# One-column operations merged on VectorE, the bias on GpSimd, and another order of the last two feed-forward steps in a state-space mixer with a quantized feed-forward network

## What is computed

```python
x = x + ssm_forward(ctx, layernorm(x))      # selective scan, 512 channels x 16 states, gated by silu(z)

def ffn(x):                                 # x = layernorm(x), 2048 rows of 512
    h = silu(bit_linear(x, w_gate)) * bit_linear(x, w_up)      # 512 -> 2048
    h = ln_weight * (h * rsqrt(mean(h * h) + 1e-6))
    return bit_linear(h, w_down)                               # 2048 -> 512
x = x + ffn(layernorm(x))

def bit_linear(x, w):
    s  = 127 / clip(max(abs(x), row), 1e-5)             # one scale for each row
    qx = clip(round(x * s), -128, 127) / s
    sw = 1 / clip(mean(abs(w)), 1e-5)                   # one scale for the matrix
    qw = clip(round(w * sw), -1, 1) / sw
    return qx @ qw.T
```

## Time and profile before

| | before |
|---|---|
| median of 3 runs | 584.28 us |
| profiled execution | 586.31 us |
| its span | 584.4 us |
| PE busy | 541.3 us (93%) |
| LDWEIGHTS (PEld) busy | 404.7 us (69%) |
| DVE busy | 540.5 us (92%) |
| ACT busy | 512.1 us (88%) |
| POOL busy | 464.5 us (79%) |
| chain that ended last | DVE 28%, PE 26%, ACT 17%, POOL 12%, issue 11%, DMA 5% |

### The profile page before, as it was taken

How to read it: one execution, slowest core, us unless ns; L and a number is a source line. 1 busy time by engine, 2 the same in 40 slices (tenths; PEclk the granted TensorE clock), 3 DMA queues, 4 the chain that set the end, 5 groups by cost and what they waited for, 6 DMA issues and landing times.

```text
span 584.4 us, 10287 instructions
## 1 busy us (share of the span) xinstructions
PE 541.3 (93%) x3667; PEld 404.7 (69%) x3684; DVE 540.5 (92%) x820; ACT 512.1 (88%) x755; POOL 464.5 (79%) x184
## 2 busy tenths in 40 slices
PE   5898987999999999999999888998889999999996
PEld 2335476899998989989999888995334444444442
DVE  3999979999999999999999999997998999999873
ACT  1899999999999999989999799998967868778673
POOL 4888374999999899999999999994564765666662
PEclk9999999999999999999999899899999999999998
DMA  9992690221112741127331194234532533424321
GB/s 285 407 364 73 230 309 11 56 65 64 55 55 91 163 117 65 59 63 202 88 98 55 55 228 168 62 128 106 104 65 63 109 81 78 112 65 97 94 54 55
DMA packets 62194, 68.65 MB, mean 117 GB/s; under 512 B 41136, under 2 KB 41136, under 8 KB 59968
## 3 DMA queue, kind: packets, MB, share of 16 engines
q1 hardware_dynamic: 59776, 63.59, 36.3%
q0 software_dynamic: 2368, 4.40, 4.5%
HBM read 50.02 MB, written 8.52 MB: 100 GB/s over the span
## 4 chain that ended last, share of the span: by engine, by line
DVE 28%; PE 26%; ACT 17%; POOL 12%; issue 11%; DMA 5%; SPq 0%; DVEq 0%; POOLq 0%; ACTq 0%
POOL arena L470 11%; ACT arena L682 8%; PE ps L1221 8%; PE ps L1205 6%; ACT arena L607 5%; DVE arena L808 5%; PE ps L1208 4%; PE ps L1263 4%; PE ps L1256 3%; DVE arena L897 3%; DVE arena L985 3%; DMA arena<-arena 2%; DVE bst_x L840 2%; DVE am L954 1%; DMA arena<-x 1%
## 5 line engine op out<-in xcount | busy, mean ns | idle before, releaser
L470 POOL TENSOR_TENSOR arena<-arena 128x2048 f32<-128x2048 f32 x63 | 286.4, 4592 | 13.2 <-DVE arena L897 11.1
L897 DVE TENSOR_TENSOR_SCAN arena<-arena,ps 128x512 f32<-128x512 f32 x256 | 286.7, 1197 | 2.0 <-ACT arena L682 0.5
L682 ACT ACTIVATE arena<-arena,a_neg 128x512 f32<-128x512 f32 x256 | 165.5, 712 | 9.5 <-DVE arena L897 9.2
L1221 PE MATMUL ps<-ident,arena 128*128 128x128 f32 x1024 | 156.0, 276 | 6.7 <-POOL arena L470 3.4
L1221 PEld LDWEIGHTS ps<-ident,arena 128*128 128x128 f32 x1024 | 121.2, 142 | 10.7 <-POOL arena L470 6.2
L504 POOL TENSOR_TENSOR arena<-arena 128x1024 f32<-128x1024 f32 x30 | 71.1, 2371 | 57.2 <-DVE arena L985 57.2
L1256 PE MATMUL ps<-arena 128*128 128x512 bf16 x504 | 112.9, 379 | 2.1 <-DVE arena L985 1.1
L1205 PE MATMUL ps<-arena 128*128 128x128 f32 x768 | 102.3, 276 | 3.4 <-ACT arena L607 2.1
L1208 PE MATMUL ps<-ident,arena 128*128 128x128 f32 x640 | 97.8, 277 | 5.2 <-DVE arena L897 2.9
L607 ACT ACTIVATE arena<-arena,bT 128x512 f32<-128x512 f32 x160 | 102.0, 711 | 0.0
L1205 PEld LDWEIGHTS ps<-arena 128*128 128x128 f32 x768 | 93.3, 192 | 5.2 <-ACT arena L607 2.3
(11 more groups left out here) (121 smaller groups left out, 578.1 us busy)
## 6 DMA issues: line engine op xcount, KB each, us to landing
arena<-w_all SPq DMA_DIRECT2D x16, 1024.0 KB, 9.2
arena<-c_rows SPq DMA_DIRECT2D x64, 256.0 KB, 3.2
arena<-x SPq DMA_DIRECT2D x4, 1024.0 KB, 15.8
w_ternary<-arena SPq DMA_DIRECT2D x8, 512.0 KB, 4.2
arena<-w_ternary SPq DMA_DIRECT2D x8, 512.0 KB, 5.0
arena<-x POOLq DMA_DIRECT2D x4, 1024.0 KB, 10.0
out<-arena SPq DMA_DIRECT2D x16, 256.0 KB, 2.0
arena<-ctx_t SPq DMA_DIRECT2D x4, 512.0 KB, 13.7
```

Source lines behind the costliest of these rows:

```text
L470: nc.gpsimd.tensor_tensor(hs[:, k % RING, :, :], hs[:, k % RING, :, :], c_bc[:, s:s + 1, :].to_broadcast([P, KE, L]), ALU.mult).then_inc(S ...
L682: nc.scalar.activation(dA[:, s, i, :], delta_u[:, b, 0, i, :], ACT.Exp, scale=a_neg[:, i, n:n + 1]).then_inc(S["dA_ready"], 1)
L897: nc.vector.tensor_tensor_scan(out=hs[:, k % RING, i, :], data0=dA[:, k % 2, i, :], data1=ps[:, 4 + i, :], initial=0.0, op0=ALU.mult, op1= ...
L1221: last = mm(ps[:, c, i * P:(i + 1) * P], hs[:, k % RING, i, c * P:(c + 1) * P], ident[:], start=(n == 0 and i == 0), stop=(n == DS - 1), i ...
```

## The change

- `variance`: the Square on ACT now takes `scales[:, t, 1:2]` as its scale from SBUF (the sum of squares then comes out scaled), and one `tensor_scalar` makes the variance of h where two did. In the end part the same is done for `var_end` and `ssq_end`.
- `scale_row`: three one-column instructions behind the reduction in place of five: clip and division by 127 in one, the two weight scales in one of two columns, and the reciprocal of the result, without the product with 127 behind it. The reciprocal itself raises `s1_ready`.
- `bias` of tiles 3 to 15 moves from DVE to POOL, behind `power` and ahead of `weigh`; it waits for POOL's own `power` and for the norm of the tile before. `bn_aggr` on DVE now waits for the bias of the tile before.
- In the last step PE makes the last quarter of gate and up ahead of down of tile 13. DVE multiplies that quarter ahead of the maximum and of q2 of tile 14, ACT makes its silu ahead of the rounding of p2 of tile 14.
- `scale_rows(13)` on ACT moves from step 15 behind the rounding of p2 of tile 15.
- The last tile's rows get a place of their own, `o_end`, and the wait for an earlier store ahead of L1063 is gone.

```diff
@@ -130,6 +130,7 @@
         sq_out = part(120, 4).bitcast(BF16)
+        o_end = part(124, 2)
@@ -378,7 +379,7 @@
                     sp.wait_ge(S["fin_done"], t + 1)
-                sp.dma_start(out_v[:, t, :], o_s[:, t % 2, :]).then_inc(out_stored[t % 2], 16)
+                sp.dma_start(out_v[:, t, :], o_end if t == END else o_s[:, t % 2, :]).then_inc(out_stored[t % 2], 16)
@@ -482,6 +483,12 @@
+            def bias(t):
+                pool.wait_ge(S["rstd_ready"], t + 1)
+                hold(pool, "xn_ready", t)
+                nc.gpsimd.tensor_scalar(bia[:], mv[:, 0:1], rstd2[:, 0:1], -1.0, ALU.mult,
+                                        ALU.mult).then_inc(S["bias_ready"], 1)
+
@@ -519,6 +526,8 @@
                     power(EARLY + t + 1, 0 if tile(t + 3) else 1, 2 if tile(t - 1) else 1)
+                if tile(t + 3):
+                    bias(t + 3)
@@ -735,7 +744,7 @@
                     hold(act, "h_ready", t * 4, "ssq_ready", t - 1)
-                    nc.scalar.activation(sq_out, h2[:, 1 - s, :], ACT.Square,
+                    nc.scalar.activation(sq_out, h2[:, 1 - s, :], ACT.Square, scale=scales[:, t - 1, 1:2],
@@ -748,21 +757,24 @@
                     nc.scalar.activation(sq_out[:, 0:1024], h2[:, END % 2, 0:1024], ACT.Square,
+                                         scale=scales[:, END, 1:2],
                                          accum_out=ssq[:, END:END + 1]).then_inc(S["ssq_ready"], 1)
+                if t == END:
+                    silu(t, 3)
...
                     round_x(t + 2)
-                if tile(t):
+                if tile(t) and t < END:
...
                     norm(t + 3)
-                if tile(t - 2):
+                if tile(t - 2) and t < END:
...
             hold(act, "h_ready", END * 4 + 4)
-            nc.scalar.activation(sq_out[:, 1024:], h2[:, END % 2, 1024:], ACT.Square,
+            nc.scalar.activation(sq_out[:, 1024:], h2[:, END % 2, 1024:], ACT.Square, scale=scales[:, END, 1:2],
@@ -773,6 +785,7 @@
                                      scale=aq[:, END:END + 1]).then_inc(S["tq_ready"], 1)
+            scale_rows(END - 2)
@@ -911,24 +924,16 @@
                     step(nc.vector.bn_stats(bst[:], x_all[:, n, :]))
+                    hold(dve, "bias_ready", n)
...
                     dve.wait_ge(S["ssq_ready"], chain + 1)
-                    own.done(nc.vector.tensor_scalar(var2[:, 1:2], ssq[:, chain:chain + 1], scales[:, chain, 1:2],
-                                                     1.0 / INNER, ALU.mult, ALU.mult))
+                    own.done(nc.vector.tensor_scalar(var2[:, 1:2], ssq[:, chain:chain + 1], 1.0 / INNER, RMS_EPS,
+                                                     ALU.mult, ALU.add))
...
                 if n is not None:
-                    own.done(nc.vector.tensor_scalar(var2[:, 0:1], mv[:, 1:2], LN_EPS, None, ALU.add))
-                if chain is not None:
-                    own.done(nc.vector.tensor_scalar(var2[:, 1:2], var2[:, 1:2], scales[:, chain, 1:2], RMS_EPS,
-                                                     ALU.mult, ALU.add))
-                own.wait()
+                    step(nc.vector.tensor_scalar(var2[:, 0:1], mv[:, 1:2], LN_EPS, None, ALU.add))
                 dve.sem_inc(S["var_ready"], 1)
-
-            def bias(n):
-                dve.wait_ge(S["rstd_ready"], n)
-                nc.vector.tensor_scalar(bia[:], mv[:, 0:1], rstd2[:, 0:1], -1.0, ALU.mult,
-                                        ALU.mult).then_inc(S["bias_ready"], 1)
@@ -952,14 +957,9 @@
                 step(nc.vector.tensor_reduce(out=am[:], in_=xn(x), axis=AX.X, op=ALU.max, apply_absolute_value=True))
-                step(nc.vector.tensor_scalar(am[:], am[:], Q_EPS, None, ALU.max))
-                own.done(nc.vector.reciprocal(s1[:], am[:]))
-                for w in range(2):
-                    own.done(nc.vector.tensor_scalar(scales[:, x, w:w + 1], wmean[:, w:w + 1], am[:], 1.0 / 127.0,
-                                                     ALU.mult, ALU.mult))
-                own.wait()
-                step(nc.vector.tensor_scalar(s1[:], s1[:], 127.0, None, ALU.mult))
-                dve.sem_inc(S["s1_ready"], 1)
+                step(nc.vector.tensor_scalar(am[:], am[:], Q_EPS, 1.0 / 127.0, ALU.max, ALU.mult))
+                step(nc.vector.tensor_scalar(scales[:, x, :], wmean[:, 0:2], am[:], None, ALU.mult))
+                nc.vector.reciprocal(s1[:], am[:]).then_inc(S["s1_ready"], 1)
@@ -994,7 +994,9 @@
                     if b == NB - 1 and n % 4 == 2 and t < EARLY:
-                        bias(t + 1)
+                        dve.wait_ge(S["rstd_ready"], t + 1)
+                        nc.vector.tensor_scalar(bia[:], mv[:, 0:1], rstd2[:, 0:1], -1.0, ALU.mult,
+                                                ALU.mult).then_inc(S["bias_ready"], 1)
@@ -1021,11 +1023,10 @@
                     scale_row(x_row)
-                if tile(t + 3):
-                    bias(EARLY + t + 1)
...
                 if t == END:
+                    gated_up(t, 3)
@@ -1034,19 +1035,14 @@
                     cut_x(x_row)
-                gated_up(t, 3)
                 if t < END:
+                    gated_up(t, 3)
...
             dve.wait_ge(S["ssq_ready"], END + 1)
-            step(nc.vector.tensor_scalar(var_end[:], ssq[:, END:END + 1], scales[:, END, 1:2], 1.0 / INNER, ALU.mult,
-                                         ALU.mult))
-            own.done(nc.vector.tensor_scalar(var_end[:], var_end[:], scales[:, END, 1:2], RMS_EPS, ALU.mult, ALU.add))
+            step(nc.vector.tensor_scalar(var_end[:], ssq[:, END:END + 1], 1.0 / INNER, RMS_EPS, ALU.mult, ALU.add))
             dve.wait_ge(S["ssq_end_ready"], 1)
-            own.done(nc.vector.tensor_scalar(ssq_end[:], ssq_end[:], scales[:, END, 1:2], 1.0 / INNER, ALU.mult,
-                                             ALU.mult))
-            own.wait()
-            step(nc.vector.tensor_scalar(var2[:, 1:2], ssq_end[:], scales[:, END, 1:2], var_end[:], ALU.mult, ALU.add))
+            step(nc.vector.tensor_scalar(var2[:, 1:2], ssq_end[:], 1.0 / INNER, var_end[:], ALU.mult, ALU.add))
@@ -1059,8 +1055,7 @@
             dve.wait_ge(S["down_psum"], TILES)
-            dve.wait_ge(out_stored[END % 2], END // 2 * 16)
-            nc.vector.scalar_tensor_tensor(out=o_s[:, END % 2, :], in0=ps[:, DOWN_BANK[END % 2], :],
+            nc.vector.scalar_tensor_tensor(out=o_end, in0=ps[:, DOWN_BANK[END % 2], :],
@@ -1257,6 +1252,9 @@
+            def turned_by_dma(t):
+                pe.wait_ge(qT_done[t % 2], (t // 2 + 1) * 16)
+
@@ -1276,8 +1274,8 @@
                         gate_and_up(t, j)
-                    if j == 2 and tile(t - 2):
-                        pe.wait_ge(qT_done[t % 2], ((t - 2) // 2 + 1) * 16)
+                    if j == 2 and tile(t - 2) and t < END:
+                        turned_by_dma(t - 2)
@@ -1288,6 +1286,8 @@
             pe.wait_ge(S["h_ready"], END * 4 + 2)
+            turned_by_dma(END - 2)
+            down(END - 2, 0, KI)
```

## The result

The changed kernel takes **589.73 us** (median of 22 runs, 583.45 to 593.77) beside 585.26 us for the kernel before on the same chip (22 runs, 583.67 to 586.6): ratio 1.0065, 95% interval 1.0043 to 1.0086. So it is slower by about 4 us, where 1.8 us less was forecast. A second set of runs gave the same: 589.92 us (7 runs, 586.77 to 591.75), ratio 1.0067 [1.0043, 1.0091].

What follows compares the result with a forecast made beforehand. The prediction took a loop through DVE and ACT (10.61 us per steady step) as the bound. Its terms 0.3 + 0.6 + 0.2 + 0.7 = 1.8 us off the 584.28 median gave 582.5 us, own range 581.7 to 583.2, with rivals 580.4 to 583.9.

Steps and rivals of the forecast that it cites:

- two waited one-column operations at 0.24: `scale_row` on DVE in a steady step: 0.24 for each operation after the reduction, part of 1.92 replacing 2.37, saving 0.45.
- slower: Outcome of a measurably slower kernel: chance 0.05, the worse half of a rival with a second clock fall (+ 3.2, 585.7 us).
- Scan stage, - 0.3: First `scale_row` call, DVE scanning without a gap: 0.30 saved reaches POOL's 0.96 wait in full, bounds 0 and - 0.4.
- Start, - 0.6 (- 1.2 with a normal landing): Start of feed-forward: q2 of tile 1 ready 0.6 earlier; - 0.6 if its transposing DMA takes 5.93, - 1.2 if 4.35.
- rival 5: Start of feed-forward: the early transposing DMA lands normally, - 0.6 more; within the forecast's range, no chance of its own.
- Step 10.59: Steady feed-forward step: 10.61 less 0.11 on DVE plus 0.09 for Square; eight steps - 0.2 us, bounds - 1.0 and + 1.1.
- 10.4 would refute the loop: Test for steady steps: the loop through DVE and ACT sets 10.59, so a measured step of 10.4 would refute it.
- DVE idle by about 0.4 ahead of L917: Steady step: the 0.45 saved in `scale_row` becomes DVE idle time of some 0.4 waiting for ACT.
- bias on POOL 0.25: POOL's extra one-column instruction: 0.25 with the wait, bounds 0.21 and 0.67; nothing in steady steps, 0.2 later in step 1.
- The end, - 0.7, or - 2.3 if the clock holds: Last step: down of tile 14 starts 0.66 earlier, gaining 0.7 at the low clock, 2.3 at the full clock.
- rival 1: Under down of tile 14 the clock holds: down takes 3.45, the end gains 2.3 instead of 0.7, 580.9 us; chance 0.28.
- parts of faster: Chances of a measurably faster kernel: 0.22 from the forecast, 0.28 and 0.08 from two rivals, given as 0.56 together.

Runs made afterwards that it cites:

- merge_only: The kernel before with only the merged operations (variance, Square, `scale_row`, end part), bias still on DVE, old order at the end: 589.02 us, ratio 1.0039.
- first_single: The changed kernel with the two columns of `scales` made by two one-column operations for tile 0 alone: 584.32 us, ratio 0.9960.
- single: The changed kernel with the two-column operation on `scales` put back to two one-column ones for all tiles: 582.84 us, ratio 0.9947.
- two_only: The kernel before with nothing changed but the two one-column operations on `scales` made one of two columns: 592.71 us, ratio 1.0118.
- single_scan: The changed kernel with one-column operations on `scales` in the scan stage (tiles 0 to 2) only, two-column ones later: 582.32 us, ratio 0.9949.
- merge_single: The kernel before with the merged operations, but `scales` by two one-column operations, bias on DVE, old order at the end: 582.38 us, ratio 0.9942.
- end_only: The kernel before with only the new order of the last step and `o_end`: 585.31 us, ratio 0.9999.
- pool_bias_only: The kernel before with only the bias moved from DVE to POOL: 585.88 us, ratio 0.9996.
- plain_square: The changed kernel with one-column operations on `scales` everywhere and no scale operand on ACT's full Square: 581.08 us, ratio 0.9917.
- whole_again: The changed kernel run once more without alteration, against the kernel before: 589.92 us, ratio 1.0067.

## Why the prediction was wrong

**The step that failed** is the one on `scale_row`: "two waited one-column operations at 0.24", which costed the merged operation, 128 x 2, like a 128 x 1, and from that "0.30 saved, less than the 0.96, so all of it arrives" in the scan stage, the term of - 0.3. Neither the forecast nor any of the five rivals had an operation held by another engine. The row behind the 0.24 was a one-column operation, the only kind that the kernel before has there, and it bounded a form that it does not cover. In its place the runs show 4.9 to 5.3 us at the first call in the three traces that lost the race, and in the changed kernel 1.60 and 1.64 at the second and third, where the shortest of these operations took 0.23 (`merge_only`, first call). From the medians: race at the first call 589.73 - 584.32 (`first_single`) = 5.4; the two later ones 584.32 - 582.84 (`single`) = 1.5; the sum is about 7, as in `two_only`. By the ratios, each to its own chip's kernel before, the two parts are 6.1 and 0.8; so the second is not resolved, the first is. The range (580.4 to 583.9) has no place for it, and slower had a chance of 0.05.

The other steps, by the traces. Pieces of the span: to the layer statistics of tile 3, to the rounding of p2 in step 4, eight steps, to that of tile 14, to the end:

| | before | changed (583.49) | `single_scan` | `merge_single` |
|---|---|---|---|---|
| to statistics of tile 3 | 404.98 | 406.11 | 404.90 | 406.23 |
| to step 4 | 43.45 | 41.97 | 41.98 | 41.73 |
| eight steps | 84.90 | 84.16 | 84.17 | 84.17 |
| to rounding of tile 14 | 31.04 | 31.40 | 31.02 | 30.44 |
| to the end | 20.03 | 17.96 | 17.93 | 18.73 |
| span | 584.4 | 581.6 | 580.0 | 581.3 |

- *Scan stage, - 0.3:* not resolved. `single_scan` is 0.08 below before, but the clock's falls lie at different places and are not as many in each trace (before 328 and 366, changed and `single_scan` 344 alone, `merge_single` 103, 328 and 397, and it comes 1.3 later than `single_scan`). The sign shows in POOL's wait: 0.64 ahead of its product at 346.52 in the first trace, where 0.96 was read and 0.7 forecast. With the two columns the piece is + 1.1 even where the first race is won.
- *Start, - 0.6 (- 1.2 with a normal landing):* - 1.5. The mechanism was right, and rival 5 came in: down of tile 1 at 435.23 waits for no DMA. The late landing (5.78 to 5.94) is in the trace of before and of `end_only`, `pool_bias_only` and `two_only`, and in none with the merged variance (4.24 to 4.39).
- *Step 10.59:* 10.52. The Square was right to the hundredth (1995 ns for 1906 + 92). The DVE side was mis-sized (0.18 saved from L917 to L972, not 0.11): L931 has numbers where L917 had a pointer operand and takes 0.15 instead of 0.21, so L931 to L935 is 0.19, not 0.24, and L935 to L972 0.29, not 0.31. Eight steps give - 0.74 instead of - 0.2. "10.4 would refute the loop" did not happen, and `plain_square` confirms it.
- *DVE idle by about 0.4 ahead of L917:* 0.35; *bias on POOL 0.25:* 0.265, hidden, as forecast.
- *The end, - 0.7, or - 2.3 if the clock holds:* in the changed kernel's trace rival 1's clock came in (- 2.1 in the last piece, with 0.4 lost ahead of it). But the new order is not needed for it. In `merge_single`, where the old end also meets a full clock, the last two pieces are 49.17, in `single_scan` 48.95: 0.2 is what the new order is worth there. At the low clock they are 51.0 in `whole_again` and 50.8 in `merge_only`, so the 0.7 that the forecast has for this case does not show either. `end_only` (0.9999 [0.9983, 1.0014]) and the pair 582.38 and 582.84 show no gain, but their intervals are too wide to exclude 0.7. The clock's fall was taken as a property of the order, and it comes and goes between executions of either order.
- *Two slips in the prediction's figures:* rival 1 takes 3.45 for down at the full clock, where the earlier trace rows have 3.62 and 3.63 and the trace after has 3.63; and its parts of faster (0.22, 0.28, 0.08) add up to 0.58, not 0.56. Neither changes which step failed.
- Without the hold the sum of the forecast, - 1.8, stands against ratios of 0.9942 to 0.9949, which is - 3.0 to - 3.4 us.

## What to carry to other kernels

Merging two tiny operations into one wider one is not free where GpSimd works beside VectorE: a `tensor_scalar` of two or three fp32 columns between SBUF tiles was held until GpSimd's running instruction ended, which costs up to the length of that instruction and not that of the operation. Keep such operations one column wide, or put them where GpSimd is idle, and cost every added shape by a row of that shape. If the times of a kernel fall into two groups, look for two engines' starts within some hundredths of a microsecond of each other, and don't trust one profiled execution: here it was of the rare group. The version to keep is `merge_single` or `single_scan` (582.4 and 582.3 us, ratios 0.9942 and 0.9949), which no run here tells apart.

## What was unexpected of the hardware

- A `tensor_scalar` of 128 x 2 or 128 x 3 fp32 values took 5.26 to 5.34 us beside a GpSimd product that started 0.33 to 0.37 after it by the records: the engine with the earlier recorded start was the one held. Of 128 x 1, 32 of 32 took 204 to 218 ns, the two at 360.69 inside a running product.
- The same gap on PE (1.96) ahead of the same matmuls was followed by the full clock in one execution (3.63 for 16 matmuls) and by half of it in another (5.31). Which it will be can't be read from the gap alone; why was not tried.
- A one-column `tensor_scalar` with numbers alone (L931) took 0.15 where one with a pointer operand (L917) took 0.21.
- Open: why the transposing DMA of tile 1's q2 lands late (5.93) in the old rhythm and not in the merged one; it was not tried.
